# Merging and advancing the attention normalisation on VectorE, and moving one small TensorE transpose ahead of its projection work

## The reference

```python
q = (Q @ Wq.T + bq).reshape(b, s, H, DH).transpose(0, 2, 1, 3)   # Q = layernorm(x)
k = (K @ Wk.T + bk)...   ;  v = (V @ Wv.T + bv)...               # K = V = ctx
scores = einsum('bhqd,bhkd->bhqk', q, k) * SCALE                 # masked, causal
attn = softmax(scores);  out = einsum('bhqk,bhkd->bhqd', attn, v)
x = x + tanh(g_xattn) * (out @ Wo.T + bo)
xk, xr = mixes of layernorm(x) with its previous token
x = x + tanh(g_ffn) * sigmoid(xr @ W_r.T) * (relu(xk @ W_k.T)**2 @ W_v.T)
```

## Time and profile before

| | |
|---|---|
| median of three runs | 2038.24 us |
| the profiled execution's own time | 2038.13 us |
| its span, first to last instruction | 2036.4 us |
| PE busy | 1932.5 us, 95% of the span |
| DVE busy | 1379.0 us, 68% |
| POOL busy | 1295.2 us, 64% |
| ACT busy | 971.1 us, 48% |
| granted clock of PE, mean | 0.98 of full |

### The profile page before, as it was taken

How to read it: one execution, slowest core, us unless ns; L and a number is a source line. 1 busy time by engine, 2 the same in 40 slices (tenths; PEclk the granted TensorE clock), 3 DMA queues, 4 the chain that set the end, 5 groups by cost and what they waited for, 6 DMA issues and landing times. The chain is left out here.

```text
span 2036.4 us, 36616 instructions
## 1 busy us (share of the span) xinstructions
PE 1932.5 (95%) x11648; PEld 1501.0 (74%) x11648; DVE 1379.0 (68%) x3534; ACT 971.1 (48%) x1870; POOL 1295.2 (64%) x1829
## 2 busy tenths in 40 slices
PE   5899999999999999999999999995599999999999
PEld 3677777777777777777777777772488888888887
DVE  3777777776777767777677777764466575656663
ACT  3555555555555555555555555544243433334341
POOL 4566666666666666666666666656277787777771
PEclk8999999999999999999999999996799999999999
DMA  5545555455554455545555445552122323132211
GB/s 182 108 114 123 128 144 124 113 123 126 144 123 114 122 128 144 118 119 121 129 144 118 118 123 127 126 145 64 62 83 82 103 72 113 67 106 74 98 67 62
DMA packets 128665, 229.31 MB, mean 113 GB/s; under 512 B 18656, under 2 KB 20704, under 8 KB 127616
## 3 DMA queue, kind: packets, MB, share of 16 engines
q1 hardware_dynamic: 128512, 227.43, 42.2%
HBM read 92.06 MB, written 33.59 MB: 62 GB/s over the span
## 5 line engine op out<-in xcount | busy, mean ns | idle before, releaser
L701 DVE CUSTOM_DVE_ANT_0 score_ps<-score_ps,causal 128x128 f32<-128x128 f32 (+3 forms) x1024 | 487.1, 504 | 295.1 <-PE score_ps L855 294.0
L533 ACT ACTIVATE probs<-prob_ps 128x512 f32<-128x512 f32 (+1 forms) x768 | 395.7, 527 | 412.3 <-PE prob_ps L879 209.2
L855 PE MATMUL score_ps<-k_stack,q_stack 97*128 97x128 f32 (+3 forms) x1024 | 319.5, 353 | 6.6 <-DVE least L701 2.9
L879 PE MATMUL prob_ps<-q_stack,k_stack 100*128 100x512 f32 (+3 forms) x1024 | 285.6, 320 | 20.4 <-DMA q_stack<-max_rows 14.3
L385 POOL TENSOR_SCALAR_AFFINE_SELECT probs<-probs 128x256 f32<-128x256 f32 x256 | 106.5, 416 | 271.7 <-ACT probs L533 271.7
L396 POOL TENSOR_TENSOR prob_sum<-probs 128x384 f32<-128x384 f32 x256 | 263.9, 1031 | 0.0
L855 PEld LDWEIGHTS score_ps<-k_stack,q_stack 97*128 97x128 f32 x1024 | 189.4, 191 | 53.5 <-issue 13.3
L879 PEld LDWEIGHTS prob_ps<-q_stack,k_stack 100*128 100x128 f32 x1024 | 193.6, 192 | 42.8 <-DMA q_stack<-max_rows 19.1
L399 POOL TENSOR_TENSOR prob_sum<-prob_sum,probs 128x256 f32<-128x256 f32 x256 | 188.8, 738 | 36.7
L389 POOL TENSOR_SCALAR_AFFINE_SELECT probs<-probs 128x256 f32<-128x256 f32 x256 | 105.0, 410 | 157.0 <-ACT probs L533 156.8
L896 PE MATMUL value_ps<-probs,v 128*32 128x512 f32 (+3 forms) x2048 | 154.8, 443 | 13.2 <-POOL prob_sum L399 13.2
(11 more groups left out here) (145 smaller groups left out, 4918.0 us busy)
## 6 DMA issues: line engine op xcount, KB each, us to landing
k_stack<-staged_k_high SPq DMA_DIRECT2D x256, 128.0 KB
q_stack<-staged_q_high SPq DMA_DIRECT2D x256, 128.0 KB, 3.1
tiles<-in_x SPq DMA_DIRECT2D x16, 1024.0 KB, 5.7
k_stack<-staged_k_low SPq DMA_DIRECT2D x128, 128.0 KB
q_stack<-staged_q_low SPq DMA_DIRECT2D x128, 128.0 KB, 3.2
x_io<-in_x SPq DMA_DIRECT2D x16, 1024.0 KB, 7.2
x<-x_io SPq DMA_DIRECT2D x64, 256.0 KB, 3.3
wk_low_room<-x SPq DMA_DIRECT2D x16, 1024.0 KB, 5.5
```

Source lines behind the costliest of these rows:

```text
L533: nc.scalar.activation(probs[:, u % RING, lo:hi], prob_ps[(3 * u + c) % 2][:, 0:hi - lo], ACT.Exp, scale=SCALE).then_inc(exp_done, 1)
L701: nc.vector.tensor_tensor_reduce(out=here, in0=here, in1=causal[:, LATE - P * t:S], scale=-1.0, scalar=3e38, op0=ALU.add, op1=ALU.min, acc ...
L855: last = nc.tensor.matmul(here[:, at:at + P * (t + 1)], q_stack[n][0:MASK_ROW + 1, j, P * t:P * t + P], k_stack[n][0:MASK_ROW + 1, j, 0:P ...
L879: last = nc.tensor.matmul(here[:, at:at + width], k_stack[n][0:ROWS, j, P * k:P * k + P], q_stack[n][0:ROWS, j, P * k:S], start=True, stop ...
```

## The change

- PE: `turn_maxima` stands at once behind `probabilities(u, 0)` in every even slot, ahead of `values` and of the first gap's work.
- PE: `project_o` waits once, at its very first step, for all four `attn_low` of the sequence.
- DVE: `correct` and `refine` are one function, both run in fourth of the slot with i % 4 == 0. `normalise` moves to second of the slot with i % 4 == 1, and `low_part_attn` to third of that slot.
- ACT: `high_part_attn` moves from fourth to second of the slot with i % 4 == 1, ahead of exponent 1.
- DVE: the layernorm statistics are two in fourth of s = 2 and two in fourth of s = 3; the aggregation stays at s = 4.

```diff
--- before.py
+++ after.py
@@ -582,6 +582,8 @@
                     apply_layernorm(b + 1, 2 * (s - 6))
                 if i % HG == 0 and 0 <= i - VALUES < N:
                     log_sums((i - VALUES) // HG)
+                if i % HG == 1 and s != 9 and 0 <= i - VALUES < N:
+                    high_part_attn((i - VALUES) // HG)
 
             def third(i, b, s):
 
@@ -604,8 +606,6 @@
                     high_part_k(b, {1: 1, 5: 2, 9: 3}[s])
                 if has_next and s == 13:
                     high_part_k(b + 1, 0)
-                if i % HG == 1 and s != 9 and 0 <= i - VALUES < N:
-                    high_part_attn((i - VALUES) // HG)
                 if has_next and s == 10:
                     high_part_x(b + 1, 2)
                 if has_next and b >= 0 and s in (11, 12):
@@ -711,12 +711,10 @@
                 nc.vector.tensor_tensor(split_max[:, PAIR * T:2 * PAIR * T], least[:, q % 2, :],
                                         split_max[:, 0:PAIR * T].bitcast(F32), ALU.subtract).then_inc(max_split, 1)
 
-            def correct(G):
+            def refine(G):
 
                 dve.wait_ge(inverted, G + 1)
                 nc.vector.tensor_tensor(sum_ps[:], sum_ps[:], inverse[:], ALU.mult).then_inc(corrected, 1)
-
-            def refine(G):
                 dve.wait_ge(corrected, G + 1)
                 nc.vector.scalar_tensor_tensor(out=inverse[:], in0=sum_ps[:], scalar=-2.0, in1=inverse[:], op0=ALU.add,
                                                op1=ALU.mult).then_inc(refined, 1)
@@ -761,13 +759,10 @@
                     low_part_x(b + 1, 2)
                 if now and s == 12:
                     low_part_attn(K * b)
+                if has_next and b >= 0 and s == 4:
+                    aggregate_stats(b + 1)
                 if i % HG == 1 and 0 <= i - VALUES < N:
-                    refine((i - VALUES) // HG)
-                if i % HG == 2 and s != 10 and 0 <= i - VALUES < N:
-                    low_part_attn((i - VALUES) // HG)
-                if has_next and b >= 0 and s == 4:
-                    layernorm_stats(b + 1, 3)
-                    aggregate_stats(b + 1)
+                    normalise((i - VALUES) // HG)
 
             def third(i, b, s):
 
@@ -776,14 +771,12 @@
                     low_part_q(b, {1: 1, 5: 2, 9: 3}[s])
                 if has_next and s == 13:
                     low_part_q(b + 1, 0)
-                if i % HG == 1 and 0 <= i - VALUES < N:
-                    normalise((i - VALUES) // HG)
-                if has_next and b >= 0 and s == 3:
-                    layernorm_stats(b + 1, 0)
                 if has_next and s == 10:
                     low_part_x(b + 1, 0)
                 if has_next and s == 11:
                     low_part_x(b + 1, 3)
+                if i % HG == 1 and s != 9 and 0 <= i - VALUES < N:
+                    low_part_attn((i - VALUES) // HG)
 
             def fourth(i, b, s):
 
@@ -791,14 +784,14 @@
                 if 0 <= i < N and i % 2 == 1:
                     split_maxima(i // 2)
                 if i % HG == 0 and 0 <= i - VALUES < N:
-                    correct((i - VALUES) // HG)
+                    refine((i - VALUES) // HG)
                 if has_next and s == 10:
                     low_part_x(b + 1, 1)
                 if has_prev and s in (6, 7):
                     add_output(b - 1, s - 6)
-                if has_next and b >= 0 and s == 3:
-                    layernorm_stats(b + 1, 1)
-                    layernorm_stats(b + 1, 2)
+                if has_next and b >= 0 and s in (2, 3):
+                    layernorm_stats(b + 1, 2 * (s - 2))
+                    layernorm_stats(b + 1, 2 * (s - 2) + 1)
                 if i == 1:
                     split_weights(3, "o")
                 if i in (N - 1, N, N + 1):
@@ -951,8 +944,8 @@
             def project_o(b, m, k):
                 if k == 0:
                     free_bank(f"o{m}", b)
-                if m == 0:
-                    pe.wait_ge(attn_low, K * b + k + 1)
+                if k == 0 and m == 0:
+                    pe.wait_ge(attn_low, K * (b + 1))
                     pe.wait_ge(w_low, 4)
                 last = exact_product(nc, bank(f"o{m}")[:], lambda k: [part[:, k, P * m:P * m + P] for part in attn],
                                      lambda k: [part[:, k, :] for part in w["o"]], [k], k == 0, k == K - 1)
@@ -992,13 +985,11 @@
                     scores(i, 0)
                 if then:
                     probabilities(u, 0)
-                if 2 <= i <= N and i % HG == 0:
+                if 2 <= i <= N and i % 2 == 0:
                     turn_maxima(i // 2 - 1)
                 if i % HG == 0 and 0 <= i - VALUES < N:
                     values((i - VALUES) // HG)
                 work(b, s, 0)
-                if 2 <= i <= N and i % HG == 2:
-                    turn_maxima(i // 2 - 1)
                 if now:
                     scores(i, 1)
                 if then:
```

## The result

| | before | after |
|---|---|---|
| median | 2038.18 us (4 runs) | 2067.94 us (4 runs, 2059.41 to 2068.76) |
| ratio of the comparable runs | | 1.014, 95% interval 1.0112 to 1.0169 |
| span of the profiled execution | 2036.4 us | 2063.6 us |
| PE busy | 1932.5 us | 1938.8 us |
| DVE busy | 1379.0 us | 1356.5 us |

The forecast was 2065 us. The changed kernel is slower by 1.4%, with VectorE less busy than before (the median `low_part_attn` takes 0.74 us instead of 1.22, since those of heads 2 and 14, which ran beside POOL's additions, now run at heads 1 and 13 without them) and PE with the same matmuls.

The account below looks back on a forecast made before the run. PE bounds the kernel and every new wait costs its full length: 1.61 us per sequence times 15 is 24.2, with the end 26.3, on 2038.1 gives 2064.4, say 2065 us. Own range 2052 to 2078, wider range 2042 to 2082.

Parts of the forecast that it names:

- Head 2: Turn on PE at head 2: waits 0.95 us for DVE's split, which runs beside POOL's sum.
- rival 1: Worse collisions at heads 2 and 14: copy and subtraction caught by POOL's two sums, 1.2 us more per sequence, 2083 us; chance 0.13.
- Heads 5 and 6: PE waits 0.40 us at head 5 for the maxima behind refine, 0.45 us at head 6 for the turn's split.
- Head 9: scores(u, 2) waits 0.40 us behind refine at head 9; heads 9 and 10 together still win 0.40 us.
- Head 13: scores(u, 2) at head 13 waits 0.36 us for maxima made later by refine beside correct.
- Head 14: Turn at head 14 waits for a split that may meet POOL's sum: bounds 0 and 0.73 us, taken as 0.35.
- Head 1's DMA wait: PE's wait at head 1 for the DMA of the maxima goes: 0.50 us won per sequence, bounds 0 and 0.85.
- The end of attention: Last sequence's output projection: nine matmuls now stand behind project_o's wait, costing 2.1 us once.
- the prediction's other case: At the end of attention the nine matmuls run at 1.2 GHz and cost 3.8 us.
- The rival that I drew from it: Head 2's split starts in front of POOL's sum, ends in 0.17 us, and head 2 loses 0.18 instead of 0.95 us.
- rival 3: Gains and losses cancel across heads, as at 2 and 14: 2047 us, or 2038 to 2042 with more won; chance 0.13.
- rival 2: Faster: waits at head 10 and the DMA wait go, up to 1.4 us won per sequence, 2019 us; chance 0.14.

Follow-up runs that it names:

- e1: The kernel before with only the turn moved at once behind the first transposed scores in every even slot; 2046.88 us, ratio 1.0052.
- e2: The kernel before with only the VectorE and ScalarE chain of the change, turn, statistics and project_o's wait as before; 2043.44 us, ratio 1.0042.
- e4: The kernel before with only the layernorm statistics moved as in the change; 2033.97 us, ratio 0.9998.
- e3: The changed kernel with the turn put back behind the first gap's work in slots with i % 4 == 2; 2042.76 us, ratio 1.0037.
- e6: The changed kernel with refine split from correct and put back in the next slot, directly ahead of normalise; 2070.53 us, ratio 1.0178.
- e7: The changed kernel with POOL's first sum cut from 384 to 16 columns at heads with u % 4 == 2; 2051.13 us, ratio 1.0078.
- e9: e8 with the split moved ahead of normalise at head 9 and ahead of the x tile's low part at head 11; 2010.06 us, ratio 0.9875.
- e8: The kernel before with the statistics as in the change and the turn early at head 14 alone; 2027.80 us, ratio 0.9971.
- e5: The kernel before with only project_o's single wait for all four attn_low; 2087.60 us, ratio 1.0267.

## Why the prediction was right

**The bound held.** PE, with every new wait at full price. The spans differ by 27.2 us; the fourteen full steps give 23.0 of it and the last sequence 2.8.

**The sum per sequence** was 1.61 us and is 1.68. Step by step, each against its stretch in the table:

- Head 2, 0.95 predicted, 1.16 measured. The mechanism held, but the caught operation changed. In e1, with VectorE's order as before, the number is 0.95 exactly, and there the DMA wait at head 1 is gone as well; so it is not this alone that changes it. In the full change `low_part_attn` stands ahead of the split as well. The prediction let VectorE's idle 0.77 us at head 1 take it up, but that idle time comes from the DMA wait, which it counted as gone. So the copy starts 0.22 behind PE's matmul instead of 0.22 ahead of it, behind the start of POOL's sum, and is caught instead of the subtraction. In two of fourteen sequences of the changed kernel the DMA wait at head 1 lasts 0.58 and 0.76 us; in these the subtraction is caught, and the turn comes 1.17 behind instead of 1.39. A wait of 0.43 us, as in the sequence shown above, is not enough for that. Catching the copy is the first half of rival 1. Its second half, a catch by POOL's second sum as well, did not come: the subtraction went through the 0.14 us gap.
- Heads 5 and 6, 0.40 + 0.45 predicted; +0.14 and +0.54 in the table. Head 5's wait is there (e2: 0.50 in that stretch), but head 4's turn no longer waits 0.3 us; I had carried this only as a bound of the statistics. That win needs the statistics and the chain together (e4 against e3). At head 6, 0.44 is the wait in the median; the remaining 0.10 comes with the turn in front of the projection, as the last section says.
- Head 9, 0.40 predicted, 0.47 measured, and the turn of head 10 with the projection, -0.80 predicted, -0.85 measured. Net -0.40 against -0.37, unrounded.
- Head 13, 0.36 predicted, 0.39 measured.
- Head 14, 0.35 predicted from bounds of 0 and 0.73; 0.04 measured. The middle between two cases was no estimate: the split either meets the sum or it doesn't.
- Head 1's DMA wait, -0.50 predicted. The stretch won only 0.23: e1 shows 0.69 for the DMA, and 0.43 us of that is lost again to the wait of `scores(1, 2)`, since with `refine` moved back (e6) the stretch is 10.59 instead of 11.02. I had put this wait at nothing as long as PE is late by the DMA, and in the same sum counted the DMA wait as gone: the two terms exclude each other.

So four terms (head 2, head 4 with 5, head 14, head 1) were off by 0.2 to 0.3 us each, two in each direction, and cancelled. That the sum came within 0.07 us is luck; the waits and the win at heads 2, 5, 6, 9, 10 and 13 were right in kind and near in size. The total has luck too: 15 sequences were counted alike, while the last one cost 2.80 us instead of 1.68 and the start of attention was 0.53 shorter. Why the last one cost more is not shown. Other executions of the changed kernel took 2059.41 to 2068.76 us, so the total itself is not sharper than some us.

**The end of attention**, 2.1 us predicted, 1.93 measured: from the last matmul of the row sums (`sum_ps<-probs,ones`) to the first of the channel mix it is 21.87 us before and 23.80 after, and 21.84, 21.75 and 21.88 in e1, e2 and e4, which have the old waits. (The 1.76 above also holds what lies ahead of it.) In the kernel after, the twelve matmuls of output tile 0 stand behind the wait:

```profile
1454.14 0.77 PE L54 MATMUL proj_ps<-wo_high,attn_high 128*128 128x512 f32 x1 [5.16 <-issue]
```

The idle time is 5.16 us where it was 2.85, the nine matmuls being what filled the difference. Around the wait's end the granted clock is at 0.50 for 3.4 us, but so it is in the kernel before, and the 3.8 us of the prediction's other case did not come.

**The rule of the Trainium skill** (SBUF — State Buffer, section "SBUF: two separate sides"), that whoever comes first holds the shared port pair for a whole instruction, agrees with what the changed kernel and e7 show: 0.99 against 0.17 us for the copy with POOL's sum long or short, and POOL's mask of 0.75 instead of 0.41 us beside VectorE's `low_part_attn`. The prediction told it for operations with two SBUF inputs; the copy has one and is held all the same. The rival that I drew from it, a split in front of the sum at head 2, did not happen in the change, but it is how e9 wins at head 10.

**The rivals.** No cancellation (rival 3) and no gain (rival 2), though the gain at head 10 was there in full (0.85) and outweighed by head 2 (1.16). That combining the parts other than in the change makes the kernel faster is shown by e8 and e9.

What stays open: whether head 2 could be made to pay less with the early turn, by moving POOL's sum instead of VectorE's split. e7 shows what the sum costs there, 0.74 us, but leaves out part of it; moving it was not tried.

## What to carry to other kernels

When one engine is full and the others wait for it in turn, an operation may be moved forward only to where its input is ready; read the end of the producer against the new place, sequence position by sequence position, because the same edit cost 1.2 us at one head and nothing at another. A tiny VectorE operation on SBUF that others wait for belongs where GpSimd is idle, or ahead of longer VectorE work that GpSimd doesn't hold up (here `normalise`, 0.68 us beside POOL's mask). And a lateness that is taken out of one wait comes back in the next, as long as the late engine has the same work to do up to there; at head 10 of e6 it came back larger, since the earlier time met a collision.

## What was not expected of the hardware

The copy of 128x8 elements with a single SBUF input (L709) was held by POOL's addition like the subtraction with two (0.99 us, undisturbed 0.17). The first 512-column matmul behind the turn is followed 0.31 us later, not 0.23 (759.01 to 759.32 in the kernel after). This isn't the wait: at head 14, where the turn doesn't wait, it is 0.31 as well, and at head 2, with the longest wait, 0.28. So a turn directly in front of a projection costs up to 0.1 us more than one in front of the scores; why is not shown. After a wait of 2.1 us (e5) the granted clock fell to its lower level in eight of fourteen sequences. And a dependent VectorE operation starts 0.03 us behind its producer's end (754.03 to 754.06) while an independent one starts 0.09 ahead of its predecessor's end (799.32 against 798.72 + 0.69 in the kernel after), so that putting a producer and its consumer side by side costs 0.12 us.
